# Six places instead of four for the parts of q and k in DRAM, and one load for each stack and half

## The chip, the cores and the metric

The kernel runs on one core of a Trainium2 chip. The metric is the device time of one execution in microseconds (us). TensorE is PE, VectorE is DVE, ScalarE is ACT, GpSimd is POOL and SyncE is SP. A name with a q behind it (SPq, POOLq, ACTq) is the sequencer of that engine as it issues a DMA.

## The reference

A block of layers works on 2,048 tokens of width 128, in this order (`_ln` is a layernorm):

```python
x = x + _L0_attn_a_ref(_layernorm(x), ...)     # a running softmax sum and a gated product
x = x + _L0_ffn_ref(_layernorm(x), ...)        # "f": two layers, L = 2
x = x + _L0_attn_b_ref(_layernorm(x), ...)     # "b": full attention, 16 heads of 8
x = x + _L0_ffn_ref(_layernorm(x), ...)        # "g": the same two layers again

# in _L0_ffn_ref, for each layer:
q = (x @ wq + bq).reshape(Bb, T, H, hd)        # H = 16 heads, hd = 8; k and v alike
att = jnp.einsum('bhqd,bhkd->bhqk', q, k) * hd ** (-0.5)
att = jnp.where(causal, att, -jnp.inf)
y = jnp.einsum('bhqk,bhkd->bhqd', jax.nn.softmax(att), v)
x = x + y @ wo + bo
x = x + moe(_ln(x), ...)                       # 8 experts of 512, the best 2
```

So there are five attentions: f0 and f1 (causal), b (full), g0 and g1 (causal).

## The kernel before

Tokens are taken in four chunks of 512. The products q k are wanted in nearly full precision from bf16 operands. So q and k are each cut into three bf16 parts, high (0), mid (1) and low (2), and six products of parts are summed: TensorE contracts over a stack of 6 x 8 = 48 rows (six pairs of parts, 8 dims of a head). A stack holds heads of even number on partitions 0 to 47 (half b = 0) and of odd number on partitions 64 to 111 (b = 1); row 48 of a half takes the shift of the softmax, so the scores contract over 49.

The way from the projection to the stacks goes through DRAM (`q_dram` and `k_dram`, shown as q_parts and k_parts), since rows have to change partitions:

- `write_part(sp, c, k, part)` (for f1 and g1 `EarlyProjection.write`) writes one part of q or k of chunk c, from 128 partitions, into every slot that holds this part. A copy into one slot is 128 x 512 bf16, 128 KB. `Q_SLOTS` and `K_SLOTS` say which part each of four slots holds; six copies of the parts would be wanted in a stack's order, and the two that are missing are read again.
- `load_stacks(queue, c, b)` (`EarlyProjection.load`) waits until all three parts of the chunk are written (`written`), and reads a half of both stacks: for each stack 32 rows (the four slots), then 16 rows again (`AGAIN`, from slot `Q_AGAIN` or `K_AGAIN`). A DMA of 32 rows moves 256 KB and one of 16 rows 128 KB. It is called for 4 chunks x 2 halves x 5 attentions.

Who issues what, in the order of each queue:

- f0, b and g0 have a projection of their own (`project_qkv` for f0 and b, `project_behind` for g0). SP writes the parts of chunks 0 to 3 in turn; behind the high parts of chunk 1 it loads chunk 0 (b = 0), behind those of chunk 2 chunk 1 (b = 0). ACT loads chunk 0 (b = 1) between its work on chunk 1. POOL loads chunk 1 (b = 1). The other loads are issued by SP and POOL at the start of the attention; in b all at once.
- ACT's cast of the high part of chunk c (L824, L821 or L1109) waits until chunk c - 2 is written, since `parts` has two buffers.
- In g0, POOL issues its load of chunk 1 ahead of the powers (`first_rows.powers`, L855) on which the normalisation of chunk 3 waits.
- The attention's order on TensorE is fixed (`plan.tensor`): `scan` (L1696, the maxima are then taken by VectorE), `turn`, `scores` (L1734) and `values` (L1755). A scan of chunk p waits until both halves of that chunk are in. The first scores wait for the first shift, a DMA by SP (L1928) that stands in SP's queue behind all writes of the projection.
- In the causal attentions POOL masks the diagonal blocks (L1917). Behind 4 and 8 masks in f0 and g0, and behind 12 and 16 in f1 and g1, it stops to issue a load.
- f1 and g1 have the projection of chunks 0 to 2 inside the expert stage ahead (`EarlyProjection`).

Of the kernel before, what the change touches and what calls it, by code (L numbers as in the profile page):

```python
# [21 lines left out]
HEADS, HD = 16, 8  # L22
# [11 lines left out]

Q_SLOTS = [0, 1, 2, 0]
K_SLOTS = [2, 1, 0, 0]
SLOTS = len(Q_SLOTS)
Q_AGAIN, K_AGAIN = 0, 1  # L40
AGAIN = 2
STACK = (SLOTS + AGAIN) * HD
PAIRS = HEADS // 2
HALF = P // 2
SHIFT_ROW = STACK
VD = HD + 1
# [581 lines left out]
def project_qkv(nc, m, n, buffers, layer=None, first_rows=None):  # L628
# [6 lines left out]
    with ExitStack() as ctx:  # L635
# [34 lines left out]
        def write_part(sp, c, k, part):  # L670

            dram, parts_of = ((m.q_dram, Q_SLOTS), (m.k_dram, K_SLOTS))[k]
            places = [g for g, of in enumerate(parts_of) if of == part]
# [6 lines left out]
        def load_stacks(queue, c, b):  # L680

            cols = slice(c * CH, (c + 1) * CH)
            for k, (stack, dram, arrived, again) in enumerate(((m.q_stack, m.q_dram, m.q_in, Q_AGAIN),
                                                               (m.k_stack, m.k_dram, m.k_in, K_AGAIN))):
                queue.wait_ge(written[k][c % 2], 16 * 3 * (c // 2 + 1))
                if c == CHUNKS - 1:
                    queue.wait_ge(v_ready, CHUNKS)
                at = HALF * b
                for n, first in ((SLOTS, 0), (AGAIN, again)):
                    queue.dma_start(stack[at:at + n * HD, c, :, :],  # L690
                                    dram.rearrange("r (hp b) s -> r b hp s", b=2)[first * HD:(first + n) * HD, b, :, cols])\
                        .then_inc(arrived[b][c], 16)
                    at += n * HD

        @block.gpsimd
        def _(pool):
            if first_rows:
                first_rows.powers(pool, BACK, 2)
            else:
                inverse_root(nc, pool, m, m.rstd[:, :], tmp[:, 0, :], var_ready, rstd_ready, 1)  # L700
            m.clear(pool, "finish", "experts", "rows", "w2")
            buffers.pad(nc, m)
            load_stacks(pool, 1, 1)

        @block.sync
        def _(sp):
            for c in range(CHUNKS):
                for part, ready in enumerate((high_ready, mid_ready, low_ready)):
                    for k in range(2):
                        sp.wait_ge(ready, 2 * c + k + 1)  # L710
                        write_part(sp, c, k, part)
                    if part == 0 and 0 < c <= EARLY:
                        load_stacks(sp, c - 1, 0)
# [87 lines left out]
        def _(act):  # L801
# [13 lines left out]
            for c in range(CHUNKS):  # L815
                for k in range(2):
                    act.wait_ge(mixed if mixing else qk_ready, 2 * c + k + 1)
                    if c >= 2:
                        act.wait_ge(written[k][c % 2], 16 * 3 * (c // 2))
                    if mixing:  # L820
                        nc.scalar.activation(parts[:, c % 2, k, 0, :], projected(c, k), ACT.Copy)\  # L821
                            .then_inc(high_ready, 1)
                    else:
                        nc.scalar.activation(parts[:, c % 2, k, 0, :], projected(c, k), ACT.Identity, bias=bias[k])\  # L824
                            .then_inc(high_ready, 1)
                if c == 1:
                    load_stacks(act, 0, 1)
                if c + 2 < CHUNKS:
                    copy_chunk(c + 2)
                for k in range(2):  # L830
                    act.wait_ge(rest_ready, 2 * c + k + 1)
                    nc.scalar.activation(parts[:, c % 2, k, 1, :], rest[:, k, :], ACT.Copy).then_inc(mid_ready, 1)
# [73 lines left out]
def project_behind(nc, m, n, buffers, layer, first_rows, attended, finish):  # L906

    src, end = m.x, CHUNKS - 1
    with ExitStack() as ctx:
# [26 lines left out]
        def write_part(sp, c, k, part):  # L936

            dram, parts_of = ((m.q_dram, Q_SLOTS), (m.k_dram, K_SLOTS))[k]
            places = [g for g, of in enumerate(parts_of) if of == part]
# [7 lines left out]
        def load_stacks(queue, c, b):  # L947

            cols = slice(c * CH, (c + 1) * CH)
            for k, (stack, dram, arrived, again) in enumerate(((m.q_stack, m.q_dram, m.q_in, Q_AGAIN),  # L950
                                                               (m.k_stack, m.k_dram, m.k_in, K_AGAIN))):
                queue.wait_ge(written[k][c % 2], 16 * 3 * (c // 2 + 1))
                if c == end:
                    queue.wait_ge(v_ready, CHUNKS)
                at = HALF * b
                for n, first in ((SLOTS, 0), (AGAIN, again)):
                    queue.dma_start(stack[at:at + n * HD, c, :, :],
                                    dram.rearrange("r (hp b) s -> r b hp s", b=2)[first * HD:(first + n) * HD, b, :, cols])\
                        .then_inc(arrived[b][c], 16)
                    at += n * HD  # L960

        @block.gpsimd
        def _(pool):
            load_stacks(pool, 1, 1)
            first_rows.powers(pool, BACK, 2)
            pool.wait_ge(finish.measured, CHUNKS)
            for name in ("searched", "exped", "drained", "projected"):
                pool.wait_ge(*attended[name])
            for done in attended["out"]:
                pool.wait_ge(*done)  # L970
            m.zero(pool, old)
            buffers.pad(nc, m)
            pool.wait_ge(m.named["h_padded"], len(buffers.layouts))
            pool.sem_inc(m.reset, 1)

        @block.sync
        def _(sp):
            for c in range(CHUNKS):
                for part in range(3):
                    for k in range(2):  # L980
                        if (c, part, k) == (end, 2, 1):
                            sp.wait_ge(low_ready, 2 * end + 1)
                            sp.wait_ge(m.reset, 2)
                        write_part(sp, c, k, part)
                    if part == 0 and 0 < c <= EARLY:
                        load_stacks(sp, c - 1, 0)
                    if c == 0 and part == 0:
                        finish.spread(sp, end)
                if c == 0:
                    finish.gather(sp, end)  # L990
# [136 lines left out]
class EarlyProjection:  # L1127
# [105 lines left out]
    def write(self, sp, c, k, part):  # L1233
        sp.wait_ge((self.high_ready, self.mid_ready, self.low_ready)[part], 2 * c + k + 1)
        dram, parts_of = ((self.m.q_dram, Q_SLOTS), (self.m.k_dram, K_SLOTS))[k]
        places = [g for g, of in enumerate(parts_of) if of == part]
# [5 lines left out]
    def load(self, queue, c, b):  # L1242
        m, cols = self.m, slice(c * CH, (c + 1) * CH)
        if c == 2:
            queue.wait_ge(*self.ones_back)
        for k, (stack, dram, arrived, again) in enumerate(((m.q_stack, m.q_dram, m.q_in, Q_AGAIN),
                                                           (m.k_stack, m.k_dram, m.k_in, K_AGAIN))):
            queue.wait_ge(self.written[k][c % 2], 16 * 3 * (c // 2 + 1))
            at = HALF * b
            for n, first in ((SLOTS, 0), (AGAIN, again)):  # L1250
                queue.dma_start(stack[at:at + n * HD, c, :, :],
                                dram.rearrange("r (hp b) s -> r b hp s", b=2)[first * HD:(first + n) * HD, b, :, cols])\
                    .then_inc(arrived[b][c], 16)
                at += n * HD

    def set_ones(self, pool):

# [382 lines left out]
def attention_heads(nc, m, n, buffers, projected, finish, rows_of, raw_weights, w2, stale, early, first_rows=None):  # L1640
# [7 lines left out]
    shift_moves = []  # L1648
    for g, (_, _, _, tiles) in enumerate(groups):
        shift_moves.append((2 if tiles == TPC else 4) + (shift_moves[g - 2] if g >= 2 else 0))  # L1650
    arrived = 32 * (m.layers + 1)
    m.layers += 1

    with ExitStack() as ctx:
# [21 lines left out]
        def _(pe):  # L1676
# [8 lines left out]
            def scan(i, g, p, parts):  # L1685
# [7 lines left out]
                for hp, t, width in parts:  # L1693
                    for b in range(2):
                        rows = slice(HALF * b, HALF * b + STACK)
                        last = nc.tensor.matmul(ps_scan[:, i % RING_A, b, at:at + width],  # L1696
# [22 lines left out]
            def scores(n_pair):  # L1719
# [10 lines left out]
                for i in range(QUAD // plan.banks(g)):  # L1730
                    pair = 2 * quad + k // 2 + i
                    for b in range(2):
                        rows = slice(HALF * b, HALF * b + STACK + 1)
                        last[b] = nc.tensor.matmul(ps_scores[(2 * n_pair + b) % RING_S][:, width * i + off:width * (i + 1)],  # L1734
# [1102 lines left out]
```

## Time and profile before

| | |
|---|---|
| median of 3 runs | 3041.94 us (3041.22 to 3053.21) |
| profiled execution, own time | 3046.33 us |
| its span | 3044.6 us |
| PE, DVE, ACT, POOL busy | 87%, 85%, 74%, 21% |
| mean granted clock of TensorE | 0.938 |

The span is what the trace covers, 1.7 us less than the execution's own time. Spans of time below are in us from the span's start: f0's projection stands at 125 to 157, b's at 1241 to 1279, g0's at 1912 to 1958, and the attentions of f1 and g1 begin at about 770 and 2570.

### The profile page before, as it was taken

How to read it: one execution, taken by the hardware profiler on the slowest of the kernel's cores; microseconds unless marked ns; L12 is line 12 of the kernel's file. 1: busy time of each engine (PE TensorE's matmuls, PEld its weight loads, DVE VectorE, ACT ScalarE, POOL GpSimd, SP SyncE). 2: the span in 40 equal slices, each digit the busy share in tenths (PEclk: the TensorE clock that was granted, in tenths of full speed). 3: DMA queues.
4: the chain of work that ended last, by engine and by line, in shares of the span. 5: the costliest groups of instructions: out<-in, count | busy, mean ns of one | idle time of the engine just before them, and what ended most of it. 6: DMA issues, size and time to landing. Idle time of an engine off the chain costs nothing. (4 is left out here: it accounts for less than half of the span.)

```text
span 3044.6 us, 71512 instructions
## 1 busy us (share of the span) xinstructions
PE 2646.6 (87%) x28144; PEld 1160.3 (38%) x28144; DVE 2598.8 (85%) x3528; ACT 2249.2 (74%) x4330; POOL 637.5 (21%) x1177
## 2 busy tenths in 40 slices
PE   3679999899799995689999999589999898899976
PEld 3432333677323334322222222232334775333325
DVE  4789998787899985799999999598997887899976
ACT  1258988676589884369999999378887675688874
POOL 5233211544321011100000000132102433321011
PEclk8779999999799997889999999799999998899998
DMA  1141000224300000410000000510001223300001
GB/s 34 53 101 39 27 23 16 73 56 97 71 27 16 18 9 24 116 27 11 17 9 17 9 16 9 138 33 29 15 13 34 66 66 89 65 28 16 13 16 28
DMA packets 109883, 119.09 MB, mean 39 GB/s; under 512 B 20726, under 2 KB 87660, under 8 KB 109548
## 3 DMA queue, kind: packets, MB, share of 16 engines
q1 hardware_dynamic: 102444, 98.21, 12.2%
q0 software_dynamic: 4608, 13.96, 2.2%
q8 instruction: 222, 3.64, 0.5%
q10 hardware_dynamic: 2496, 2.36, 0.3%
q14 instruction: 113, 0.93, 0.1%
HBM read 70.31 MB, written 43.78 MB: 37 GB/s over the span
## 5 line engine op out<-in xcount | busy, mean ns | idle before, releaser
L1804 ACT ACTIVATE h_probsg<-h_ps_lowg 128x512 f32<-128x512 f32 (+3 forms) x812 | 424.5, 551 | 108.5 <-PE h_ps_lowg L1734 70.7
L1804 ACT ACTIVATE h_probsf<-h_ps_lowf 128x512 f32<-128x512 f32 (+3 forms) x812 | 424.4, 550 | 107.3 <-PE h_ps_lowf L1734 68.5
L1804 ACT ACTIVATE h_probsb<-h_ps_lowb 128x512 f32<-128x512 f32 x683 | 389.2, 596 | 61.0 <-PE h_ps_lowb L1734 46.2
L1755 PE MATMUL h_ps_valuesg<-h_probsg,v_all 128*9 128x256 f32 (+2 forms) x4608 | 350.2, 376 | 25.9 <-POOL h_probsg L1917 19.0
L1755 PE MATMUL h_ps_valuesf<-h_probsf,v_all 128*9 128x256 f32 (+2 forms) x4608 | 349.0, 375 | 26.0 <-POOL h_probsf L1917 19.3
L1755 PE MATMUL h_ps_valuesb<-h_probsb,v_all 128*9 128x256 f32 x4096 | 317.9, 382 | 7.9 <-ACT h_drainedb L1813 3.1
L1856 DVE TENSOR_REDUCE h_maxima_0b<-h_ps_scanb 128x2 f32<-128x1024 f32 x256 | 292.5, 1213 | 6.7 <-PE h_ps_scanb L1696 6.7
L1856 DVE TENSOR_REDUCE h_maxima_2b<-h_ps_scanb 128x2 f32<-128x1024 f32 x256 | 292.6, 1214 | 5.1 <-PE h_ps_scanb L1696 5.1
L1856 DVE TENSOR_REDUCE h_maxima_0g<-h_ps_scang 128x2 f32<-128x1024 f32 x224 | 258.9, 1216 | 19.8 <-PE h_ps_scang L1696 19.1
L1856 DVE TENSOR_REDUCE h_maxima_0f<-h_ps_scanf 128x2 f32<-128x1024 f32 x224 | 258.6, 1216 | 18.6 <-PE h_ps_scanf L1696 18.0
L1804 ACT ACTIVATE h_probsf<-h_ps_highf 128x512 f32<-128x512 f32 (+3 forms) x404 | 224.0, 554 | 35.0 <-PE h_ps_lowf L1734 32.3
L1804 ACT ACTIVATE h_probsg<-h_ps_highg 128x512 f32<-128x512 f32 (+3 forms) x404 | 224.0, 555 | 34.7 <-PE h_ps_lowg L1734 32.2
L1917 POOL TENSOR_SCALAR_AFFINE_SELECT h_probsg<-h_probsg 128x128 f32<-128x128 f32 (+1 forms) x384 | 121.5, 330 | 610.9 <-ACT h_probsg L1804 603.8
L1917 POOL TENSOR_SCALAR_AFFINE_SELECT h_probsf<-h_probsf 128x128 f32<-128x128 f32 (+1 forms) x384 | 121.5, 330 | 574.9 <-ACT h_probsf L1804 568.2
L1696 PE MATMUL h_ps_scanf<-k_stack,q_stack 48*128 48x512 bf16 (+3 forms) x1280 | 217.5, 360 | 25.4 <-DVE h_maxima_0f L1856 7.9
L1696 PE MATMUL h_ps_scang<-k_stack,q_stack 48*128 48x512 bf16 (+3 forms) x1280 | 219.8, 364 | 22.6 <-DVE h_maxima_0g L1856 7.3
L1734 PE MATMUL h_ps_lowf<-q_stack,k_stack 49*128 49x256 bf16 (+2 forms) x1368 | 226.9, 286 | 10.3 <-DMA q_stack<-h_shiftsf 4.4
L1734 PE MATMUL h_ps_lowg<-q_stack,k_stack 49*128 49x256 bf16 (+2 forms) x1368 | 228.0, 287 | 7.8 <-ACT h_probsg L1804 2.6
L1696 PE MATMUL h_ps_scanb<-k_stack,q_stack 48*128 48x512 bf16 x1024 | 202.8, 393 | 21.6 <-DVE h_maxima_0b L1856 9.4
L1804 ACT ACTIVATE h_probsb<-h_ps_highb 128x512 f32<-128x512 f32 x341 | 203.4, 596 | 11.1 <-PE h_ps_lowb L1734 8.2
L1734 PE MATMUL h_ps_lowb<-q_stack,k_stack 49*128 49x256 bf16 x1366 | 200.2, 275 | 5.9 <-ACT h_probsb L1804 5.6
L1856 DVE TENSOR_REDUCE h_maxima_2g<-h_ps_scang 128x2 f32<-128x1024 f32 x160 | 185.5, 1218 | 14.5 <-PE h_ps_scang L1696 13.5
(465 smaller groups left out, 5240.6 us busy)
## 6 DMA issues: line engine op xcount, KB each, us to landing
q_stack<-combine_weights SPq DMA_DIRECT2D x64, 256.0 KB, 3.7
q_stack<-in_L_ffn_e_w SPq DMA_DIRECT2D x24, 256.0 KB, 3.3
q_stack<-q_parts SPq DMA_DIRECT2D x22, 256.0 KB, 5.5
k_stack<-k_parts SPq DMA_DIRECT2D x22, 256.0 KB, 7.4
attended<-h_drainedf SPq DMA_DIRECT2D x16, 256.0 KB, 2.3
attended<-h_drainedf SPq DMA_DIRECT2D x32, 128.0 KB, 2.0
attended<-h_drainedb SPq DMA_DIRECT2D x32, 128.0 KB, 1.9
attended<-h_drainedg SPq DMA_DIRECT2D x16, 256.0 KB, 2.3
```

Source lines behind the costliest of these rows:

```text
L1696: last = nc.tensor.matmul(ps_scan[:, i % RING_A, b, at:at + width], m.q_stack[rows, c, 2 * quad + hp, t * P:(t + 1) * P], m.k_stack[rows, ...
L1734: last[b] = nc.tensor.matmul(ps_scores[(2 * n_pair + b) % RING_S][:, width * i + off:width * (i + 1)], m.k_stack[rows, kb // TPC, pair, at ...
L1755: last = nc.tensor.matmul(ps_values[32 * j:32 * j + VD, low:high], m.v_all[:, kb, QUAD * quad + j, :], probs[:, (u + j % banks) % RING_P, ...
L1804: nc.scalar.activation(by_head(probs[:, of % RING_P, :], of), by_head(ps_scores[of % RING_S], of), ACT.Exp, scale=SOFTMAX_SCALE).then_inc( ...
L1856: nc.vector.tensor_reduce(found[:, :, low], now, AXIS_X, ALU.max).then_inc(freed, 1)
L1917: nc.gpsimd.affine_select(out=at, in_=at, compare_op=ALU.is_ge, fill=0.0, base=0, pattern=[[0, at.shape[1]], [1, P]], channel_multiplier=- ...
```

## The change

Six slots take the place of four, in the order of the stack's pairs, so that all 48 rows of a half are one run of rows. A part's copies are 3, 2 and 1 (high, mid, low) instead of 2, 1 and 1, for q and for k alike. The second DMA of each load goes. The six pairs of parts are the same, in another order. A stack's semaphore counts 16 for a layer instead of 32.

```diff
-Q_SLOTS = [0, 1, 2, 0]
-K_SLOTS = [2, 1, 0, 0]
+Q_SLOTS = [0, 0, 0, 1, 1, 2]
+K_SLOTS = [2, 0, 1, 0, 1, 0]
 SLOTS = len(Q_SLOTS)
-Q_AGAIN, K_AGAIN = 0, 1
-AGAIN = 2
-STACK = (SLOTS + AGAIN) * HD
+STACK = SLOTS * HD
...
         def load_stacks(queue, c, b):
 
             cols = slice(c * CH, (c + 1) * CH)
-            for k, (stack, dram, arrived, again) in enumerate(((m.q_stack, m.q_dram, m.q_in, Q_AGAIN),
-                                                               (m.k_stack, m.k_dram, m.k_in, K_AGAIN))):
+            for k, (stack, dram, arrived) in enumerate(((m.q_stack, m.q_dram, m.q_in),
+                                                               (m.k_stack, m.k_dram, m.k_in))):
                 queue.wait_ge(written[k][c % 2], 16 * 3 * (c // 2 + 1))
                 if c == CHUNKS - 1:
                     queue.wait_ge(v_ready, CHUNKS)
-                at = HALF * b
-                for n, first in ((SLOTS, 0), (AGAIN, again)):
-                    queue.dma_start(stack[at:at + n * HD, c, :, :],
-                                    dram.rearrange("r (hp b) s -> r b hp s", b=2)[first * HD:(first + n) * HD, b, :, cols])\
-                        .then_inc(arrived[b][c], 16)
-                    at += n * HD
+                queue.dma_start(stack[HALF * b:HALF * b + STACK, c, :, :],
+                                dram.rearrange("r (hp b) s -> r b hp s", b=2)[:, b, :, cols]).then_inc(arrived[b][c], 16)
...
-    arrived = 32 * (m.layers + 1)
+    arrived = 16 * (m.layers + 1)
```

`load_stacks` of `project_behind` and `EarlyProjection.load` change in the same way.

SP's queue in f0's projection, from the high parts of chunk 1 to the high parts of chunk 2. The names are destination<-source, and the sizes are partitions or rows x copies (or head pairs) x tokens. Before:

```order
L677 DMA q_parts<-p_partsf 128x2x512
L677 DMA k_parts<-p_partsf 128x2x512
L690 DMA q_stack<-q_parts 32x8x512
L690 DMA q_stack<-q_parts 16x8x512
L690 DMA k_stack<-k_parts 32x8x512
L690 DMA k_stack<-k_parts 16x8x512
L677 DMA q_parts<-p_partsf 128x512
L677 DMA k_parts<-p_partsf 128x512
L677 DMA q_parts<-p_partsf 128x512
L677 DMA k_parts<-p_partsf 128x512
L677 DMA q_parts<-p_partsf 128x2x512
L677 DMA k_parts<-p_partsf 128x2x512
```

The same place in SP's queue after the change:

```order
L675 DMA q_parts<-p_partsf 128x3x512
L675 DMA k_parts<-p_partsf 128x3x512
L686 DMA q_stack<-q_parts 48x8x512
L686 DMA k_stack<-k_parts 48x8x512
L675 DMA q_parts<-p_partsf 128x2x512
L675 DMA k_parts<-p_partsf 128x2x512
L675 DMA q_parts<-p_partsf 128x512
L675 DMA k_parts<-p_partsf 128x512
L675 DMA q_parts<-p_partsf 128x3x512
L675 DMA k_parts<-p_partsf 128x3x512
```

The four load instructions became two, and the high and mid writes carry one copy more each; their number and order are as they were.

POOL's queue in an attention f1 (g1 is alike), where the last two loads stand between masks. Before:

```order
L1917 AFFINE_SELECT h_probsf<-h_probsf 128x128 x8
L1263 DMA k_stack<-k_stack 1x16x512 x2
L1917 AFFINE_SELECT h_probsf<-h_probsf 128x128 x4
L1251 DMA q_stack<-q_parts 32x8x512
L1251 DMA q_stack<-q_parts 16x8x512
L1251 DMA k_stack<-k_parts 32x8x512
L1251 DMA k_stack<-k_parts 16x8x512
L1917 AFFINE_SELECT h_probsf<-h_probsf 128x128 x4
```

The same place in POOL's queue after the change:

```order
L1903 AFFINE_SELECT h_probsf<-h_probsf 128x128 x8
L1249 DMA k_stack<-k_stack 1x16x512 x2
L1903 AFFINE_SELECT h_probsf<-h_probsf 128x128 x4
L1239 DMA q_stack<-q_parts 48x8x512
L1239 DMA k_stack<-k_parts 48x8x512
L1903 AFFINE_SELECT h_probsf<-h_probsf 128x128 x4
```

POOL has two instructions less between the masks here, and again in the load behind these four masks.

## Rows read from the trace of the kernel before

**Rows 1.** The page: the span, and busy time by engine.

```profile
span 3044.6 us, 71512 instructions
PE 2646.6 (87%) x28144; PEld 1160.3 (38%) x28144; DVE 2598.8 (85%) x3528; ACT 2249.2 (74%) x4330; POOL 637.5 (21%) x1177
```

**Rows 2.** DMA issues: out<-in, queue, count, KB each, median us from issue to landing.

```profile
q_stack<-q_parts SPq DMA_DIRECT2D x22, 256.0 KB, 5.5
...
q_stack<-q_parts SPq DMA_DIRECT2D x22, 128.0 KB, 7.1
...
q_parts<-k_stack SPq DMA_DIRECT2D x8, 256.0 KB, 2.9
q_parts<-k_stack SPq DMA_DIRECT2D x16, 128.0 KB, 1.9
```

**Rows 3.** Stretches of f0: busy time by engine, granted clock, DMA share, GB/s.

```profile
141.00:150.00 9.00, 7.00 (x26) 3.98 (x25) 6.28 (x18) 3.26 (x6) 0.00 (x0) 0.81 1.05 240
...
153.00:161.00 8.00, 3.21 (x36) 1.82 (x36) 6.40 (x8) 1.77 (x3) 1.90 (x4) 0.58 0.96 212
161.00:165.00 4.00, 2.22 (x25) 1.34 (x25) 3.97 (x6) 0.00 (x0) 2.06 (x4) 0.50 1.09 374
165.00:174.00 9.00, 5.01 (x52) 2.71 (x52) 5.38 (x7) 1.08 (x2) 0.44 (x3) 0.50 1.03 169
```

**Rows 4.** Timeline of f0: start, us, engine, instruction [idle before <-releaser].

```profile
152.25 1.26 ACT L824 ACTIVATE p_partsf<-p_ps_qkf,vecs_dh 128x512 bf16<-128x512 f32 x2 [1.14 <-DMA q_parts<-p_partsf]
...
165.16 1.48 SPq L1928 DMA_DIRECT2D q_stack<-h_shiftsf  x2
...
172.20 0.61 PE L1734 MATMUL h_ps_lowf<-q_stack,k_stack 49*128 49x512 bf16 x2 [3.04 <-DMA q_stack<-h_shiftsf]
```

**Rows 5.** Timeline of b.

```profile
1264.79 0.60 ACT L807 ACTIVATE q_stack<-p_ps_turnb 128x512 f32<-128x512 f32 x1 [2.17 <-issue]
...
1274.45 1.22 SPq L690 DMA_DIRECT2D q_stack<-q_parts  x2
...
1297.13 0.61 PE L1696 MATMUL h_ps_scanb<-k_stack,q_stack 48*128 48x512 bf16 x2 [0.85 <-DMA k_stack<-k_parts]
```

**Rows 6.** Stretches of b, columns as in rows 3.

```profile
1262.00:1272.00 10.00, 7.32 (x29) 4.26 (x30) 7.02 (x16) 4.58 (x8) 0.00 (x0) 1.00 0.96 227
...
1283.00:1287.00 4.00, 2.21 (x8) 0.41 (x8) 4.00 (x5) 0.00 (x0) 1.33 (x3) 0.50 1.08 365
1287.00:1298.00 11.00, 5.77 (x22) 1.04 (x20) 11.00 (x11) 0.00 (x0) 3.07 (x6) 0.50 1.06 211
1298.00:1304.00 6.00, 3.38 (x12) 0.55 (x12) 6.00 (x6) 0.00 (x0) 0.00 (x0) 0.50 0.93 152
```

**Rows 7.** g0: the chain that ended last (start, us, what).

```profile
1930.29 7.28 DMA q_parts<-p_partsg
...
1937.86 1.16 POOL q_stack L957 x2
1939.02 1.10 POOL k_stack L957 x2
...
1940.13 1.04 POOL rstd L855
```

**Rows 8.** g0: a stretch, columns as in rows 3.

```profile
1960.00:1969.00 9.00, 6.13 (x67) 3.43 (x67) 8.28 (x10) 0.00 (x0) 0.00 (x0) 0.50 0.00 0
```

**Rows 9.** Timelines of g1: POOL's loads, and PE's values that waited.

```profile
2593.93 1.15 POOL L1251 DMA_DIRECT2D q_stack<-q_parts  x2 [0.36 <-DMA k_stack<-k_stack]
...
2597.15 1.10 POOL L1251 DMA_DIRECT2D q_stack<-q_parts  x2
2597.25 0.41 PE L1755 MATMUL h_ps_valuesg<-h_probsg,v_all 128*9 128x128 f32 x8 [1.65 <-POOL h_probsg L1917]
2600.51 1.04 PE L1755 MATMUL h_ps_valuesg<-h_probsg,v_all 128*9 128x256 f32 x8 [0.60 <-POOL h_probsg L1917]
```

**Rows 10.** Waits of f1, 780 to 812: us in total, times, longest.

```profile
PE h_ps_valuesf L1755 <- POOL h_probsf L1917: 3.0, 3, 1.5
```

More of the change, by code:

```diff
@@ L949, in load_stacks @@
             cols = slice(c * CH, (c + 1) * CH)
-            for k, (stack, dram, arrived, again) in enumerate(((m.q_stack, m.q_dram, m.q_in, Q_AGAIN),
-                                                               (m.k_stack, m.k_dram, m.k_in, K_AGAIN))):
+            for k, (stack, dram, arrived) in enumerate(((m.q_stack, m.q_dram, m.q_in),
+                                                               (m.k_stack, m.k_dram, m.k_in))):
                 queue.wait_ge(written[k][c % 2], 16 * 3 * (c // 2 + 1))
@@ L954, in load_stacks @@
                     queue.wait_ge(v_ready, CHUNKS)
[L955 to L960, printed above, removed]
+                queue.dma_start(stack[HALF * b:HALF * b + STACK, c, :, :],
+                                dram.rearrange("r (hp b) s -> r b hp s", b=2)[:, b, :, cols]).then_inc(arrived[b][c], 16)
         @block.gpsimd
@@ L1245, in load @@
             queue.wait_ge(*self.ones_back)
-        for k, (stack, dram, arrived, again) in enumerate(((m.q_stack, m.q_dram, m.q_in, Q_AGAIN),
-                                                           (m.k_stack, m.k_dram, m.k_in, K_AGAIN))):
+        for k, (stack, dram, arrived) in enumerate(((m.q_stack, m.q_dram, m.q_in),
+                                                           (m.k_stack, m.k_dram, m.k_in))):
             queue.wait_ge(self.written[k][c % 2], 16 * 3 * (c // 2 + 1))
[L1249 to L1254, printed above, removed]
+            queue.dma_start(stack[HALF * b:HALF * b + STACK, c, :, :],
+                            dram.rearrange("r (hp b) s -> r b hp s", b=2)[:, b, :, cols]).then_inc(arrived[b][c], 16)
     def set_ones(self, pool):
```

## The prediction

> **What bounds the kernel now.** I read the page first: TensorE is busy for 87% of a span of 3044.6 us and VectorE for 85% [rows 1]. The attentions and the experts keep these two at work, and there the change does nothing: TensorE has the same instructions, on operands of the same shape. So it can only act where the program waits for parts of q and k, or for an engine that issues their DMAs. I looked for these places in the timelines, engine by engine, around each of the five attentions, then in the list of waits, and asked in the stretches how full the DMA engines are there.
>
> In f0 the DMA share is 0.96 or more in the stretches shown between 141 and 174 [rows 3]. It is full because both halves of a chunk are read at once with the writes of the next between them. Two waits hang on it: ACT's high part of chunk 3 waits 1.14 us for the writes of chunk 1, and the first scores wait 3.04 us for their shift, which was issued at 165.16 and let TensorE go at 172.20 [rows 4]. In b it is full too, from 1262 to 1304 but for a moment after 1274 [rows 6]; TensorE waits 0.85 us for chunk 2 of k at 1297.13 [rows 5]. In g0 the chain goes through the writes of chunk 1 (7.28 us), then four load instructions on POOL, then the power on which chunk 3 waits [rows 7]. In f1 and g1 the DMA engines are not the limit; POOL is, between masks [rows 9, 10].
>
> **More bytes written.** A chunk has 12 copies of 128 KB instead of 8, so 4 more, 0.52 MB; over 4 chunks and 5 attentions 10.5 MB. In the stretches in which nearly all packets are writes the engines moved 374 and 365 GB/s [rows 3, 6]. A high pair or a mid pair (q and k) has 0.26 MB more, which is 0.70 us at that rate. Other rows give the bounds: 128 KB more took a lone write from 1.9 to 2.9 us [rows 2], so 2.0 us a pair when nothing overlaps, and at the rate of a mixed stretch, 240 GB/s [rows 3], a pair is 1.1 us. Where the DMA engines are idle, the cost is nothing. I take 0.70, since a full queue shows throughput and not latency; at 1.1 each such place costs half as much again, which goes into the range.
>
> f0: in SP's queue ahead of the shift, and inside the full stretch, stand six such additions (high and mid of chunks 1, 2 and 3): 6 x 0.70 = 4.2 us. Some 0.7 us fits into the gap near 153 in which the share is a little under 1. So first scores come **3.5 us** later. On the way, chunk 1 is written 1.4 us later, and ACT's wait of 1.14 grows to about 2.5; that is a part of the 3.5 and not on top. Behind the late scores everything on TensorE is late, since its order is fixed.
>
> b: chunk 2's load stands behind the same six additions, so its landing goes from 1297.1 to 1301.3, and the scans of chunk 2 with it: **4.2 us**. VectorE works without a pause up to there, so this comes out whole. Chunk 3 is loaded behind it and scanned behind it; it moves along. ACT issues two loads less at 1262 to 1264, of the four that kept it for 2.17 us longer than its input did [rows 5], which is worth 1.2 us to the projection; but chunk 1's writes then land at about 1275.8 and hold ACT's high part of chunk 3, so the gain isn't seen.
>
> g0: chunk 1 lands later by its mid pair, 0.7 us, and by as much again for its high pair, ahead of its loads: together 1.4. POOL then needs two instructions less, of 0.55 to 0.58 us each [rows 7]: -1.1. Net **+0.3 us**. The first shift isn't touched: from 1960 to 1969 the DMA share is 0.00 [rows 8], so 1.4 us more of writes ends in idle time.
>
> **Fewer load instructions.** 80 go: half of the 160. A pair of them took 1.10 to 1.15 us on POOL [rows 9], whatever the size, so POOL wins 1.1 us for a load. In g1, values waited 1.65 and 0.60 us for POOL's masks just behind the two loads [rows 9]: the first can give back 1.1 and the second its 0.60, **-1.7 us**. f1 has 3.0 us of such waits in the same place [rows 10], among which I count the same **-1.7**. On SP the instructions go as well, but there SP waits for data or for DMAs anyway. For SP's rows of weights in the expert stages, which stand behind the loads, I give nothing.
>
> The Trainium skill, in SBUF — State Buffer, section "Door 1: The DMA port swizzle", says that partitions 32 to 47 are reached through the same ports as 0 to 15. By that rule a half puts the same load on its fullest ports in one DMA as in two, and reading would take as long as before; the sum would be the one below. The rows show a half-stack's second DMA of 128 KB landing 7.1 us after its issue, the first of 256 KB 5.5 [rows 2], and a stretch in which nearly all packets are loads at 152 GB/s [rows 6]. That is less than half of the rate of the writes, and doesn't say what one DMA of 48 rows does.
>
> **Sum.** 3.5 + 4.2 + 0.3 - 1.7 - 1.7 = +4.6 us. Against the profiled execution's own 3046.33 us (1.7 beside its span) that is 3050.9. That execution is 4.4 us over the median of the runs, 3041.94, so the median goes to about 3046.
>
> **Rivals.** *A, one load of 48 rows is faster than 32 and 16.* For it speaks that loads move at 152 GB/s and that a small DMA follows each large one. What it can give is bounded by the waits that exist: 1.14 and 3.04 in f0, 0.85 in b and 1.2 for ACT's issues there, in g0 1.1 on POOL and about 1 of the 7.28, 3.4 in f1 and g1. The loads must win back the 4.2 us first. 11.7 at most, so 3030; half way 3036. The Trainium skill's page DMA: Bandwidth & Descriptors has for this, under "Rules for kernel authors", the advice to coalesce small transfers into large ones. Against it: 128 KB isn't small, and the bytes are the same.
>
> *B, POOL's instructions give nothing in f1 and g1*, since ACT or the shift holds TensorE just behind. Then 4.2 + 3.5 + 1.4 = +9 us: 3051.
>
> *C, slower by more than noise: the read in one piece is slower*, because 48 rows fall unevenly on 16 DMA engines or ports. b has three chunks ahead of its gate, 4.7 MB, or 31 us at 152 GB/s; f0 two or so, g0 one. If the reads took 1.3 times as long, b loses 9 us, f0 6, g0 3: 18 with the 4.6 is +23, 3065. It passes 0.5% (15 us) when reads are 1.18 times as long. Nothing in the rows shows a load of 48 rows, so it can't be ruled out.
>
> *D, the change has no effect*: all the writes fit in idle time. The full shares in rows 3 and 6 speak against it; it leaves the gains of 1.1, 1.7 and 1.7, and so 3037.
>
> **How the numbers follow.** The forecast (writes cost 2 to 8 us net) has a chance of 0.57, A 0.17, B 0.13, D 0.08, C 0.05. About 0.5%, 15 us here, is what a measurement can tell from no change. Only C passes it, and A in its extreme doesn't: faster 0.02, same 0.93, slower 0.05. The likeliest is 3046. The range leaves out C and the lower half of A: 3036 to 3054. The bottom holds D. The top holds B (3051), and 1.1 us instead of 0.70 for a pair (2.4 us more in f0 and as much in b, 3051 too), with a little of both.
>
> **What would show it.** Right: in f0 the first scores near 175.7 with a longer wait for h_shifts; b's scan of chunk 2 waiting 3 us or more for k_stack; in f1 and g1 values waiting 1.7 us less for POOL; in g0 POOL's power at about 1940.4; writes of 384 KB landing about 0.7 us behind those of 256 KB. Wrong: b's scans without a wait, or loads of 384 KB that land earlier than 128 KB did before (A); loads that land more than 3 us later (C); masks that wait for ACT at 2594 (B).

## The result, and the profile after

The changed kernel takes 3057.21 us in the median of 7 runs (3051.22 to 3063.19); the kernel before takes 3050.33 on the same chip (7 runs, 3041.22 to 3053.21). The two medians differ by 6.9 us. The comparison of all runs gives a ratio of 1.0034, with a 95% interval of 1.0023 to 1.0046, or +10.4 us (7 to 14). I had forecast +4.6, and 3046 with a range up to 3054, so 3057.21 lies above the range. Within 0.5% of before it is, as forecast. The three runs of before that I was shown had a median 8.4 us lower than all seven; I took that median as the base although the profiled execution stood at 3046.33.

The page after, answering to [rows 1], and its line on DRAM traffic (HBM):

```profile
span 3049.5 us, 71432 instructions
PE 2639.9 (87%) x28144; PEld 1151.8 (38%) x28144; DVE 2601.6 (85%) x3528; ACT 2250.0 (74%) x4330; POOL 623.4 (20%) x1147
HBM read 70.31 MB, written 54.26 MB: 41 GB/s over the span
```

80 instructions are gone and 10.5 MB more are written. TensorE is busy for 6.7 us less than before, VectorE for 2.8 us more and ACT for 0.8 us more, so the 10 us must be in waits. The DMA issues after, answering to [rows 2]:

```profile
q_stack<-q_parts SPq DMA_DIRECT2D x22, 384.0 KB, 8.4
k_stack<-k_parts SPq DMA_DIRECT2D x22, 384.0 KB, 10.2
...
q_parts<-k_stack SPq DMA_DIRECT2D x8, 384.0 KB, 3.2
...
q_parts<-k_stack SPq DMA_DIRECT2D x8, 256.0 KB, 2.8
```

A lone write of q of 384 KB takes 0.4 us more to land than one of 256 KB (3.2 against 2.8); for k it is 0.8 us (3.3 against 2.5). The 0.7 that I took lies between. A load of 48 rows of q lands 8.4 us after its issue, where 32 rows took 5.5 and the 16 issued behind them 7.1.

f0 in the timeline after: a turn (the second) near the start of the projection, ACT's high part of chunk 3, the first shift, the first scores [rows 4].

```profile
126.68 1.09 PE L765 MATMUL p_ps_turnf<-ident,q_stack 128*128 128x128 f32 x4 [0.96 <-ACT q_stack L803]
...
153.45 1.26 ACT L818 ACTIVATE p_partsf<-p_ps_qkf,vecs_dh 128x512 bf16<-128x512 f32 x2 [3.98 <-DMA q_parts<-p_partsf]
...
166.36 1.48 SPq L1914 DMA_DIRECT2D q_stack<-h_shiftsf  x2
...
173.65 0.61 PE L1720 MATMUL h_ps_lowf<-q_stack,k_stack 49*128 49x512 bf16 x2 [3.29 <-DMA q_stack<-h_shiftsf]
```

The same turn before:

```profile
128.28 1.09 PE L771 MATMUL p_ps_turnf<-ident,q_stack 128*128 128x128 f32 x4 [0.96 <-ACT q_stack L809]
```

This execution was 1.6 us ahead at that turn. From there the first scores come 46.97 us later, where it was 43.92 to the first scores of [rows 4]: 3.05 us more. I call this stretch **f0's measure**.

b after: ACT's first cast of a high part, its wait for the writes of chunk 1, the first scan of chunk 2 [rows 5].

```profile
1256.83 0.60 ACT L815 ACTIVATE p_partsb<-p_ps_mixedb 128x512 bf16<-128x512 f32 x1 [4.77 <-PE p_ps_mixedb L789]
...
1278.86 1.08 ACT L815 ACTIVATE p_partsb<-p_ps_mixedb 128x512 bf16<-128x512 f32 x2 [6.43 <-DMA q_parts<-p_partsb]
...
1305.23 1.03 PE L1682 MATMUL h_ps_scanb<-k_stack,q_stack 48*128 48x512 bf16 x4 [4.74 <-DMA k_stack<-k_parts]
```

The first cast before:

```profile
1255.05 0.60 ACT L821 ACTIVATE p_partsb<-p_ps_mixedb 128x512 bf16<-128x512 f32 x1 [4.81 <-PE p_ps_mixedb L795]
```

From the first cast to the first scan of chunk 2 are 48.40 us. Before it was 42.08 (the scan at 1297.13 is in [rows 5]). I call this **b's measure**; it doesn't depend on what an execution lost earlier. It grew by 6.3 us, where I had 4.2. Counted from the first cast, SP issues its load of chunk 2 at 34.6 us instead of 30.4, and from there to the scan are 13.8 us instead of 11.7.

g0 after, POOL's loads of chunk 1 and the power [rows 7]:

```profile
1947.52 0.68 POOL L949 DMA_DIRECT2D q_stack<-q_parts  x1 [36.91 <-DMA q_parts<-p_partsg]
1948.20 0.64 POOL L949 DMA_DIRECT2D k_stack<-k_parts  x1
1948.84 1.03 POOL L849 TENSOR_TENSOR rstd<-next_tmp,neg_half 128x4 f32<-128x4 f32 x1
```

Everything is 8.5 us late when g0 begins, so the power's 1948.84 is 1940.3 counted as in the trace of before; I had forecast 1940.4. From VectorE's first instruction in g0's projection (at 1912.05 before) to the power are 28.3 us, before 28.1. But in the eight traces of this document whose g0 is that of before, this stretch runs from 27.7 to 29.8 us, so an effect of 0.3 us can't be told from one execution. f1 after, what TensorE waits for from 780 to 812 [rows 10]:

```profile
PE h_ps_highf L1720 <- DMA q_stack<-h_shiftsf: 2.1, 1, 2.1
...
PE h_ps_valuesf L1741 <- POOL h_probsf L1903: 1.0, 2, 0.6
```

The wait for masks fell from 3.0 to 1.0 us, as forecast and a little more. In its place stands a wait of 2.1 us for a shift. g1 is alike: 1.0 us for masks and 2.3 for h_shiftsg.

### The profile page after: what moved, and what is told of

Read it like the earlier page. It is cut to its first block and busy times, and to the rows that moved or that the text cites. A ratio compares the mean times of both kernels' runs of the same rounds, so it can differ in the third digit from the quotient of the medians.

```text
span 3049.5 us, 71432 instructions
## 1 busy us (share of the span) xinstructions
PE 2639.9 (87%) x28144; PEld 1151.8 (38%) x28144; DVE 2601.6 (85%) x3528; ACT 2250.0 (74%) x4330; POOL 623.4 (20%) x1147
## 3 DMA queue, kind: packets, MB, share of 16 engines
q1 hardware_dynamic: 111980, 108.69, 13.3%
## 5 line engine op out<-in xcount | busy, mean ns | idle before, releaser
L1720 PE MATMUL h_ps_lowf<-q_stack,k_stack 49*128 49x256 bf16 (+2 forms) x1368 | 227.4, 286 | 10.4 <-DMA q_stack<-h_shiftsf 4.6
```

## Experiments

All of these kernels keep the instructions of TensorE, VectorE and ACT as they are. "Four" is the layout of before, "six" that of the change. Times are given as a ratio to the kernel before, run beside it. y2_stale, y1_before_again, z1_thirds and z2_halves ran once each, so of these only the trace is read.

The measures repeat like this. b's measure is 41.79 to 42.21 us in the seven traces whose b is that of before. With the change in b it is 48.33, 48.40, 49.08 and 51.53 (x3, the change, w3, w2). f0's measure is 43.09 to 44.04 in eight traces with the f0 of before, and 45.24, 46.97, 47.08 and 47.48 in the four with the change there (w2, the change, x3, y2). So a single trace shows well that a kernel is slower than before in b, but a difference of 3 us between two of the slower ones can be chance.

### Who pays: writes, reads, places

**x2_apart.** Six places are written everywhere; the read stays two DMAs.

```diff
-    queue.dma_start(stack[at:at + 48], dram[0:48])
+    queue.dma_start(stack[at:at + 32], dram[0:32]); queue.dma_start(stack[at + 32:at + 48], dram[32:48])
```

> The six places are written as in the change, but each stack and half is still read by two DMAs, 32 rows and then 16. Theory W (the bytes written are what costs): as slow as the change or a little slower, +9 to +14 us against the kernel before, and b's first scan of chunk 2 waits 4 us or more for k_stack. Theory R (the read in one piece is what costs): no more than +4 us, since the reads are those of before. Theory G (f1 and g1 lose by the early loads): about +10 less what f1 and g1 lost, so +5 to +8, with f1 and g1 drifting by nothing.

1.0024 (1.0013 to 1.0034): +7.3 us (4 to 10). b's measure is 1303.22 - 1257.99 = 45.23 us, 3.15 more than before:

```profile
1257.99 0.60 ACT L842 ACTIVATE p_partsb<-p_ps_mixedb 128x512 bf16<-128x512 f32 x1 [4.34 <-PE p_ps_mixedb L816]
...
1303.22 1.03 PE L1715 MATMUL h_ps_scanb<-k_stack,q_stack 48*128 48x512 bf16 x4 [2.29 <-DMA k_stack<-k_parts]
```

So the bytes do cost. In b's traces they cost about half of what the change costs there, in f0 all of it: f0's measure is 47.63 us, against 46.97 with the change. The time lies between what theories W and R foresaw. It isn't told apart from the change's +10.4 (7 to 14).

**y2_stale.** In b and g0 the loads are those of the change, and the bytes written those of before: two of the six places of each stack aren't rewritten and hold what f0 left, so the scores of b and g0 are not the reference's.

```diff
-([0, 0, 0, 1, 1, 2], [2, 0, 1, 0, 1, 0])    # part in each place, q and k, in b and g0
+([0, 0, -, 1, -, 2], [2, 0, 1, 0, -, -])    # "-": read, but not written
```

> Six places in f0; in b and g0 the loads of 48 rows, but only as many copies are written as before (two of the high part, one of the mid and low part, of q and of k), so three places of each stack hold what f0 left there and b's and g0's scores are wrong; f1 and g1 as before. Theory W (only bytes written cost): b's first scan of chunk 2 waits 1 us or less for k_stack, b drifts by 0 to +0.5 us. Theory R (reading in one piece is about a tenth slower): b drifts by +2 to +4 us with the bytes written as before.

```profile
1258.91 0.60 ACT L842 ACTIVATE p_partsb<-p_ps_mixedb 128x512 bf16<-128x512 f32 x1 [3.82 <-PE p_ps_mixedb L816]
...
1305.57 1.04 PE L1715 MATMUL h_ps_scanb<-k_stack,q_stack 48*128 48x512 bf16 x4 [4.76 <-DMA k_stack<-k_parts]
```

b's measure is 46.66 us: 4.6 more than before without one more byte written. With reads of 48 rows in one DMA, chunk 2 is there later than with 32 and then 16 (theory R). The two costs don't quite add (3.15 and 4.6, together 6.3).

The end of b's DMA traffic says the same. From the first cast to the last packet of chunk 3's load, the seven traces with the b of before take 47.0 to 49.3 us for 10.5 MB, and y2_stale 52.3 for the same 10.5 MB. x2_apart takes 50.6 for 12.6 MB, and the four with the change 54.8 to 56.2 for the same 12.6 MB. Of y2's 4.6 us, 2.8 are lost before SP issues the load of chunk 2 (33.2 us behind the first cast, before 30.4) and 1.8 from there to the scan.

**x3_six_fbg, x4_six_late, w3_six_b.** Six places and one load in f0, b and g0; in f1 and g1; in b alone. Each attention chooses its layout:

```diff
+MODES = {"f0": "six", "f1": "four", "b0": "six", "g0": "six", "g1": "four"}    # x3; x4 and w3 alike
```

> Six places and one load in f0, b and g0, the four places and two loads of before in f1 and g1. Theory W: +8 to +11 us. If f1 and g1 realised their 1.7 us each, this is 3 us slower than the change; if they gave nothing, it is equal to it; by theory G it is 2 to 5 us faster than the change.

> Six places and one load in f1 and g1 alone, four places elsewhere. My prediction's -1.7 and -1.7 give -3.4 us. Rival B of the prediction (POOL's instructions give nothing): 0 within 1 us. Theory G (earlier loads delay the shift and the clock of TensorE falls there): +2 to +5 us. In the trace, the scores behind the second group's shift wait about 2 us for h_shifts in both f1 and g1.

> Six places and one load in b alone. By the traces (the first scan of chunk 2 comes 6.3 us later, b ends 5 to 6 us later): +5 to +7 us. By the prediction's term: +4.2 us. Rival (lost time in b is partly made up behind it): +2 us or less.

| six places in | ratio (95%) | us |
|---|---|---|
| f0, b, g0 | 1.0039 (1.0023 to 1.0055) | +11.9 |
| b alone | 1.0027 (1.0015 to 1.0039) | +8.2 |
| f1, g1 | 1.0008 (0.9997 to 1.0019) | +2.4 (-1 to +6) |
| all five | 1.0034 (1.0023 to 1.0046) | +10.4 |

b has most of it, +8.2 with an interval of 5 to 12. For f0 and g0 together 11.9 - 8.2 = 3.7 are left, where I had 3.8; with intervals of 4 to 5 us on either side of both, this is weak support. f1 and g1 give nothing, where I had -3.4.

### How the read is cut

**z1_thirds, z2_halves.** The change with the stacks of f0, b and g0 read by three DMAs of 16 rows, and by two of 24.

```diff
-    [(48, rows[0:48])]
+    [(16, rows[at:at + 16]) for at in (0, 16, 32)]     # z1;  z2: (24, ...) for at in (0, 24)
```

> The change, but in f0, b and g0 each stack and half is read by three DMAs of 16 rows instead of one of 48. The measure is the time in b from the first cast of a high part to the first scan of chunk 2: 42.1 us before, 48.4 with the change, 45.2 with the change's writes and reads of 32 and 16 rows. Theory N (the fewer and larger the DMAs in flight, the slower the reads): 45 us or less. Rival P (only the pattern of 48 rows over the DMA engines is bad, and 32 and 16 are as good as it gets): 45 to 46. Rival B (only bytes count): 48 as with the change.

> The change, but in f0, b and g0 each stack and half is read by two DMAs of 24 rows: as many DMAs as before, but another cut. Theory N: about 45, as with 32 and 16 rows. Rival P (rows must be dealt out in sixteens): 47 to 50 us, as bad as 48 rows in one or worse, since 24 rows do not go evenly over 16 engines.

With the writes of the change, b's measure is 45.23 us for 32 and 16 rows, 47.85 for three times 16 (1311.01 - 1263.16), 48.33 to 51.53 for 48 and 50.61 for 24 and 24 (1307.15 - 1256.54). Neither new cut reaches 45, so theory N falls in b; but neither is told from one DMA of 48 rows. In f0 the order is another: f0's measure is 44.30 for 24 and 24, 48.31 for three times 16, and 45.24 to 47.48 for 48, in single traces that I can't explain. In b the cut into 24 and 24 can be seen in the DMA share; here are two stretches of z2_halves, and behind them one of the change:

```profile
1300.00:1306.00 6.00, 0.00 (x0) 0.00 (x0) 1.25 (x2) 0.00 (x0) 0.00 (x0) 0.50 0.89 193
...
1304.00:1306.00 2.00, 0.00 (x0) 0.00 (x0) 0.00 (x0) 0.00 (x0) 0.00 (x0) 0.50 0.82 212
```

```profile
1300.00:1306.00 6.00, 1.26 (x6) 0.13 (x4) 2.21 (x3) 0.00 (x0) 0.00 (x0) 0.50 1.09 191
```

The columns are those of [rows 3]. TensorE and VectorE stand and wait for the loads, and yet the DMA share with halves is 0.89, and 0.82 in its last 2 us, where the reads of 48 rows have 1.09. The Trainium skill, in DMA: Bandwidth & Descriptors, "Why a DMA increments its semaphore by 16 and not by 1", says that a DMA runs on the largest number of engines up to 16 that divides the slowest dimension of its source and of its destination. By that rule 24 rows run on 12 of 16, and the trace agrees with it: 12/16 of 1.09 is 0.82. But the bytes moved in the 6 us are the same, 193 and 191 GB/s, so the share alone doesn't show that halves cost time. The rule makes 16 engines for 48, 32 and 16 rows alike, and so doesn't explain the other three.

**x1_overlap.** Four places, and yet one DMA of 48 rows: the source is two overlapping runs of 24 rows for q and three of 16 for k.

```diff
-Q_SLOTS, K_SLOTS = [0, 1, 2, 0], [2, 1, 0, 0]
+Q_SLOTS, K_SLOTS = [0, 0, 1, 2], [2, 1, 0, 0]
+    source = [[8 * row, n], [row, 48 // n], ...]       # n = 2 for q, 3 for k
```

> Only four places are written (q holds parts 0, 0, 1, 2 and k holds 2, 1, 0, 0), and each stack and half is read by one DMA of 48 rows whose source rows overlap (two runs of 24 rows for q, three of 16 for k, each run 8 rows behind the last). Theory W: no cost is left and POOL, SP and ACT save their instructions, -1 to -7 us against the kernel before; chunk 2 of k in b is no later than before. Theory R: +4 to +10 us, and loads of 384 KB still land 8 to 10 us after their issue in b with scans that wait. Theory G: f1 and g1 drift as in the change (gain near 802, lost again by 813), 0 to +4 in all.

1.0632 (1.0613 to 1.0652), some 190 us slower, which no theory had. The stretch from 1351, in which such a load runs:

```profile
1351.00:1361.00 10.00, 5.99 (x18) 2.72 (x17) 4.79 (x10) 2.33 (x4) 0.00 (x0) 0.95 0.19 66
```

A share of 0.19 is three sixteenths. By the same rule of the Trainium skill the source's outermost dimension, 3 for k, holds the DMA to 3 engines; the trace agrees. So this kernel told about its own source pattern, and nothing about the change.

**z3_four_thirds.** Four places, three reads of 16 rows in f0, b and g0.

```diff
-    for n, first in ((4, 0), (2, again)):
+    for n, first in ((2, 0), (2, 2), (2, again)):      # n and first in places of 8 rows
```

> Four places as before; in f0, b and g0 each stack and half is read by three DMAs of 16 rows instead of 32 and 16. Theory N: reads are faster still; b's measure falls from 42.1 to 40 or 41, where VectorE's scans of chunks 0 and 1 become the limit, and f0's first scores come 0 to 2 us earlier; against that stand 0.6 us more for each load on POOL, SP and ACT: -2 to 0 us against the kernel before. Rival P: the issues alone count, 0 to +3 us.

1.0011 (1.0002 to 1.0020), +3.4 us (1 to 6): the cut of before is better than this one too. b's measure is 44.07 us (1302.20 - 1258.13), where theory N had 40 or 41. The scan doesn't wait for its load there; the first scan of chunk 0 comes 26.1 us behind the first cast, before 24.1, so the 2 us are lost in the projection.

### f1 and g1: where the gain went

x4_six_late has the change in f1 and g1 alone. What TensorE waits for from 780 to 812, and its stretch behind 804:

```profile
PE h_ps_highf L1753 <- DMA q_stack<-h_shiftsf: 2.3, 1, 2.3
...
PE h_ps_valuesf L1774 <- POOL h_probsf L1936: 1.0, 2, 0.6
```

```profile
804.00:812.00 8.00, 7.44 (x49) 1.36 (x51) 5.13 (x6) 4.87 (x11) 2.34 (x8) 0.50 0.55 92
```

The shift is issued at 793.85, among POOL's loads of chunks 2 and 3, and lets TensorE go only at 803.89, ten us later. In that stretch the granted clock is 0.50, the lower of its two levels (1.2 GHz); before it was 1.00 there. TensorE's instruction that starts at 775.17, 800.67 and 810.41 in the trace of before starts here at 776.14, 798.35 and 811.75: 3.3 us won by 801, and lost again by 811. The next three kernels move POOL's load of chunk 3.

```diff
-                if (k - late) % 4 == 0 and 0 <= (k - late) // 4 < CHUNKS - EARLY:
-                    projected["load"](pool, EARLY + (k - late) // 4, 1)
+                load_behind = (late, 32 if early else 4)       # 24 in z4, w1 and w2
+                if k in load_behind:
+                    projected["load"](pool, EARLY + load_behind.index(k), 1)
```

> Six places and one load in f1 and g1, four places in f0, b and g0, and POOL's load of chunk 3 in f1 and g1 behind the 32nd mask. Theory S: the wait of 2.3 us for h_shifts near 802 and near 2609 goes, TensorE keeps its full granted clock there, and f1 and g1 each keep the 2.8 us that the trace without the move had won by 801 and lost by 813: -4 to -7 us against the kernel before, about 5 us faster than the same kernel without the move. Rival (the gain near 801 is given back whatever the shift does): 0 to +3 us, as without the move.

> The kernel before (four places, two DMAs) with one edit: in f1 and g1 POOL's load of chunk 3 stands behind the 32nd mask instead of the 16th, where POOL has nothing to do for 2 to 3 us. Theory S (the loads of chunks 2 and 3 in one burst hold up the shift issued in the middle of them, and POOL's issues hold up masks): POOL's issues of that load delay no mask, so values waits about 1 us less for masks in each of f1 and g1, and the shift lands well before it is wanted; -2 to -4 us. Rival: TensorE is held just behind by something else, 0 within 1.5 us.

Neither moves the time beyond its interval of some 3 to 4 us on either side: 0.9996 (0.9985 to 1.0008) for y4, 1.0000 (0.9989 to 1.0011) for y3. In y4 the wait for the shift is gone, but ACT now waits, and TensorE behind it for 2.8 us:

```profile
819.18 0.60 ACT L1832 ACTIVATE h_drainedf<-h_ps_valuesf 128x512 f32<-128x512 f32 x1 [2.61 <-DMA attended<-h_drainedf]
```

That write was issued at 810.48, behind POOL's load at 804.94 and SP's from 807.20 on. The same traffic, moved, held up another small DMA. Behind the 24th mask it lies between the two:

> Six places and one load in f1 and g1, four places elsewhere, and POOL's load of chunk 3 in f1 and g1 behind the 24th mask. Theory S (what gates f1 and g1 is a small DMA, a shift or a write of attended rows, that travels in the traffic of the loads): here that load lies between both small DMAs, so neither the 2.3 us for h_shifts nor the 2.6 us for attended is seen; values waits up to 1.3 us more for masks: -1 to -4 us. Rival (what is gained on TensorE is given back in any case): 0 within 1.5 us.

Here are TensorE's wait for masks from 780 to 820 and the stretch from 804:

```profile
PE h_ps_valuesf L1774 <- POOL h_probsf L1937: 2.1, 3, 0.8
...
804.00:812.00 8.00, 7.28 (x102) 2.67 (x94) 8.00 (x8) 5.05 (x15) 3.86 (x15) 1.00 1.03 191
```

0.9978 (0.9968 to 0.9987), -6.7 us (4 to 10). Neither small DMA is waited for, and the granted clock is 1.00 from 792 to 820. This is faster than both kernels. Is it the change or the move?

> The kernel before, with POOL's load of chunk 3 in f1 and g1 behind the 24th mask instead of the 16th. If the 6.7 us of the kernel with six places there were the move's alone: -5 to -8 us. If both are needed (POOL's shorter issues bring TensorE forward, and the move keeps the small DMAs out of the traffic that would take this back): -2 to +1 us, with 1.1 us more at each of the two loads in POOL's queue.

> The change as it is, with POOL's load of chunk 3 in f1 and g1 behind the 24th mask. f0, b and g0 cost +12 as measured with them alone, f1 and g1 give 6.7: +3 to +8 us against the kernel before, 4 to 8 us faster than the change. Rival (the two do not add, since g1's part depends on how the clock falls): within 3 us of the change's +10.

w1 has 0.9981 (0.9971 to 0.9992), -5.8 us (2 to 9 faster). So the move alone wins time, with four places too. z4's 6.7 is only 0.9 more; but with intervals of 3 us on either side of both, that can't tell nothing from the 3.4 that I had forecast for six places in f1 and g1. w2 has 1.0018 (1.0006 to 1.0030), +5.5 us (2 to 9), 4.9 less than the change; x3's +11.9 and z4's -6.7 would make +5.2, so the parts add up roughly. Its b's measure was 51.53, the highest of all; why it is 2 to 3 us over the others with the same code in b is open.

The traces say more. The table has the time in us between two instructions of VectorE in f1 (at 769.01 and 829.05 before) and two in g1 (at 2582.00 and 2699.34 before), the same ones in every trace.

| POOL's load of chunk 3 behind mask | four places: f1; g1 | six places: f1; g1 |
|---|---|---|
| 16 | 57.94 to 60.10; 117.34 to 118.53 (6 traces) | 60.00 to 60.65; 117.77 to 119.27 (4 traces) |
| 24 | 58.28; 116.38 (w1) | 56.29 and 56.33; 114.76 and 114.73 (z4, w2) |
| 32 | 61.55; 118.57 (y3) | 59.63; 115.89 (y4) |

With the load where it was, six places win nothing. With it moved they are 1.6 to 2.7 us shorter in each attention, at mask 24 by 2.0 and 1.6: about the -1.7 and -1.7 of the prediction. This rests on one to two traces a cell, and two traces of the kernel before differ by 2.1 us in f1 (60.04 and 57.94), so it is likely and not shown.

**y1_before_again.** The kernel before, traced a second time.

> The kernel before, word for word in what it issues, for a second trace to compare with: how much of a drift between two traces is from one execution to the next. If the first trace of before had lost 5 us between 2011 and 2560, as the four other traces suggest, this one is 4 to 6 us earlier than it at 2560; otherwise they agree within 1 us.

b's measure is 41.83, 0.25 from the first trace. Elsewhere two traces of the same kernel differ more. Matched instruction by instruction on TensorE, this one was 7.4 us behind the first trace at 1995 and 2.3 us at 2582. Between these points the first trace had lost 5 us or more that 11 of the 16 other traces, the changed kernel's among them, hadn't lost. Without that loss the profiled spans, which differ by only 4.9 us, would differ by about 10, as the runs do (+10.4). This is why I read single attentions from measures with both ends inside them.

## Why the prediction was wrong

**What bounds it** held: the busy time of TensorE, VectorE and ACT changed by under 7 us each, and the new waits stand at the places named in f0 and b.

**More bytes written** held as a mechanism. In b, writes alone cost 3.15 us of 4.2 forecast (x2_apart). f0 came to 3.05 of 3.5 in the first trace, and to 1.3 to 3.6 over the four with the change there. So 0.70 us for a pair was about right where the queue is full, a little high in b. That g0's power came within 0.1 us of the forecast, and f0 and g0 in time within 0.1 us (3.7 of 3.8), is luck in part: the first varies by 2 us from trace to trace, and the second is a difference of two results that are each known to 4 or 5 us.

**b: 4.2 us** is the first term that failed, with 6.3 in the trace and 8.2 (5 to 12) in time. It rested on reads that take as long in one DMA as in two; y2_stale shows 4.6 us for that step, which the sum had at nothing. I had put a slower read at 0.05, as rival C. It is rival C's effect at half the size at which C was priced: 4.6 us over the 31 us of reads that I had reckoned ahead of b's gate is 1.15 times (an estimate), and C's threshold stood at 1.18. The 31 us were too long, though. They came from 152 GB/s, a stretch in whose last 2 us the loads were running out (the DMA share is 0.69 from 1302 to 1304); from 1290 to 1298 the loads moved 190 GB/s, which makes 25 us and 1.19 times. In f0 nothing of it is seen: x2_apart, with two reads, is no faster there. What I had worked out from the Trainium skill's port rule (SBUF — State Buffer, "Door 1: The DMA port swizzle"), reads as long as before, is not borne out in b: y2_stale measures 4.6 us more. ACT's wait for the writes of chunk 1 in b did hide the issues saved, as said, and did more: chunk 3's cast (1278.86) comes 22.0 us behind the first, before 19.5, and chunk 3's writes, behind which the load of chunk 2 stands, come later with it.

**Fewer load instructions: -1.7 and -1.7** is the second. The waits for POOL fell by 2.0 and 1.7, right to a few tenths. But I counted them as won without asking what TensorE meets next. It was rival B, which named the shift. B's +9 with b's 2.1 more is +11, close to the +10.4 measured, although B also counts 1.1 us in g0 that the trace doesn't show. I gave B 0.13 although [rows 9] show the loads issued in the very window in which the shift travels; the shift's landing was a row that I hadn't looked up. The terms themselves may well be right: with the load of chunk 3 moved, the traces show 2.0 and 1.6 us for them.

**A**, the faster read, was wrong in sign in b. **D** falls with f0 and b.

**The base.** I went from the profiled execution's 3046.33 down to the median of three runs, 3041.94. Seven runs gave 3050.33, and 20 or more in each later comparison 3045.3 to 3047.2, so that median was 3 to 8 us low. From 3041.94, +10.4 would have ended at 3052.3, inside the range. So it is the base that put the measured 3057.21 above 3054. The two terms made the effect larger than forecast: 4.6 with 2.1 more for b and without the 3.4 of f1 and g1 is 10.1, near the +10.4.

**Open**: why, with one DMA of 48 rows, b's chunk 2 arrives later than with 32 and 16. The runs show only that it is so beside other traffic. A lower rate of the reads isn't seen where they run nearly alone: y2_stale moves 195 GB/s from 1300 to 1306, before 190 from 1290 to 1298. Another order in which reads and writes get their turn is a rival that no run tests.

## What to carry to other kernels

Fewer DMA instructions aren't less DMA time: measure a read in the new shape beside the traffic that it will meet before counting it as neutral. When an engine is relieved, look up the landing of each small DMA in the same window, since it travels in the traffic of the large ones; where a load stands between two of them was worth 6 us here (2 to 9), and only with the load moved do the traces show the gain of fewer instructions. Repeat the trace of a kernel before reading small differences from it: the same code in b varied by 3 us. And take the base from the same execution as the terms of the sum.

## What the runs showed of the hardware

A shift, two DMAs of 0.5 KB, took 10 us from issue to use amid loads of 384 KB (issued 793.85, used 803.89, in x4_six_late). The granted clock can fall to 0.50 in f1 without any wait for a DMA: in y3_four_moved it is 0.50 from 798 to 812, the lower of its two levels, with TensorE busy for 13.3 of 14 us; in the 6 us before that TensorE was busy for 3.8 and the clock already at 0.84. The kernel's time was that of before all the same, although TensorE waited 1.5 us less for masks in f1 (1.5 against 3.0). In z4, with the same instructions on TensorE, the clock was 1.00 from 792 to 820, although TensorE was busy for only 4.1 us from 798 to 804. What makes it fall there isn't settled. The stretch of y3 from 798, columns as in [rows 3]:

```profile
798.00:804.00 6.00, 5.88 (x60) 1.81 (x56) 2.67 (x3) 2.56 (x8) 2.26 (x8) 0.50 0.00 0
```
